# Moving one output projection inside every step of a software-pipelined attention and FFN kernel

## What is computed

```python
h = gelu(other @ W1 + readout @ W2 + b)                      # token layer
n = layernorm(h)
q, k, v = split(n @ qkv_w.T)                                 # 16 heads of 64
scores = q @ k.T * 64**-0.5 + bias[bucket(key - query)]      # T5 relative bias
h = h + (softmax(scores) @ v) @ o_w.T                        # attention
n = layernorm(h)
h = h + (silu(n @ wg.T) * (n @ wu.T)) @ wd.T                 # gated FFN, int weights / 127
```

## Time and profile before

| what | value |
|---|---|
| median of 3 runs | 1811.13 us (1810.99 to 1811.48) |
| the profiled execution's own time | 1811.56 us |
| its span, first to last instruction | 1809.3 us |
| granted TensorE clock, mean of the span | 0.99 |
| PE busy | 1766.2 us (98%) |
| PE weight loads busy | 1648.3 us (91%) |
| DVE, ACT, POOL busy | 1515.6 us (84%), 1396.9 us (77%), 1167.8 us (65%) |
| DMA queue of the loads and stores | 5.7% of 16 engines' span |
| chain that ended last | PE 95%, DVE 3%, ACT 1%, issue 1% |

### The profile page before, as it was taken

How to read it: one execution, slowest core, us unless ns; L and a number is a source line. 1 busy time by engine, 2 the same in 40 slices (tenths; PEclk the granted TensorE clock), 3 DMA queues, 4 the chain that set the end, 5 groups by cost and what they waited for, 6 DMA issues and landing times.

```text
span 1809.3 us, 47269 instructions
## 1 busy us (share of the span) xinstructions
PE 1766.2 (98%) x17434; PEld 1648.3 (91%) x17434; DVE 1515.6 (84%) x4828; ACT 1396.9 (77%) x3795; POOL 1167.8 (65%) x1488
## 2 busy tenths in 40 slices
PE   7899999999999999999999999999999999999996
PEld 5789999999999999999999999999999999999995
DVE  4888888888888888888888888888889888889884
ACT  4877778777778777787777787777787777877873
POOL 2566567666667666667666667666667666667664
PEclk8999999999999999999999999999999999999998
DMA  5200000000000000000000000000000000000000
GB/s 181 71 11 16 16 10 9 14 16 16 16 7 11 16 16 16 16 4 14 16 16 16 16 4 13 16 16 16 16 5 13 16 16 16 16 5 13 8 7 13
DMA packets 26761, 34.13 MB, mean 19 GB/s; under 512 B 3457, under 2 KB 20370, under 8 KB 26530
## 3 DMA queue, kind: packets, MB, share of 16 engines
q1 hardware_dynamic: 26368, 30.95, 5.7%
q10 hardware_dynamic: 98, 0.07, 0.0%
q0 software_dynamic: 64, 0.07, 0.0%
HBM read 22.65 MB, written 8.42 MB: 17 GB/s over the span
## 4 chain that ended last, share of the span: by engine, by line
PE 95%; DVE 3%; ACT 1%; issue 1%; POOL 0%; DMA 0%; POOLq 0%; ACTq 0%; DVEq 0%
PE ps L480 57%; PE ps L561 14%; PE ps L537 13%; PE ps L550 7%; PE ps L489 3%; PE ps L505 2%; DVE prob L958 1%; DVE pT L966 1%; ACT prob L786 0%; POOL normed L410 0%; ACT pT L793 0%; DMA emb_sb<-emb 0%; DVE wu L897 0%; ACT xt L753 0%; DVE v L944 0%
## 5 line engine op out<-in xcount | busy, mean ns | idle before, releaser
L419 POOL TENSOR_TENSOR prob<-prob,inv 128x510 f32<-128x510 f32 x512 | 524.8, 1039 | 371.6 <-DVE inv L971 371.6
L793 ACT ACTIVATE pT<-ps 128x512 fp32r<-128x512 f32 x512 | 278.5, 597 | 322.4 <-PE ps L550 322.3
L786 ACT ACTIVATE prob<-prob,neg_top 128x255 f32<-128x255 f32 x1024 | 506.8, 502 | 5.0 <-DVE neg_top L958 4.7
L958 DVE CUSTOM_DVE_ANT_0 prob<-ps,bias 128x255 f32<-128x255 f32 x1024 | 380.1, 420 | 98.8 <-PE ps L537 91.5
L480 PE MATMUL ps<-xnT,wqk 128*128 128x256 f32 x3072 | 417.0, 285 | 2.9 <-DVE qk L936 1.5
L480 PEld LDWEIGHTS ps<-xnT,wqk 128*128 128x128 f32 x3072 | 381.8, 189 | 15.2 <-issue 1.8
L966 DVE TENSOR_TENSOR pT<-ps,pT 128x512 fp32r<-128x512 f32 x512 | 334.5, 685 | 1.5 <-ACT pT L793 1.5
L561 PE MATMUL ps<-pT,v 128*128 128x256 f32 x2048 | 294.9, 287 | 20.3 <-DVE pT L966 11.2
L561 PEld LDWEIGHTS ps<-pT,v 128*128 128x128 f32 x2048 | 263.7, 190 | 37.6 <-issue 31.8
L537 PE MATMUL ps<-qk 64*128 64x256 f32 x3072 | 252.5, 297 | 0.8 <-DVE neg_top L958 0.8
L537 PEld LDWEIGHTS ps<-qk 64*128 64x128 f32 x3072 | 198.9, 186 | 35.7 <-issue 1.8
(11 more groups left out here) (93 smaller groups left out, 2592.0 us busy)
## 6 DMA issues: line engine op xcount, KB each, us to landing
xt<-x_cols SPq DMA_DIRECT2D x32, 256.0 KB, 2.6
out<-xt SPq DMA_DIRECT2D x32, 128.0 KB, 1.7
r_rows<-readout_rows SPq DMA_DIRECT2D x30, 128.0 KB, 2.9
out<-xt SPq DMA_DIRECT2D x32, 112.0 KB, 1.8
bias<-bias_rows SPq DMA_DIRECT2D x8, 384.0 KB, 4.2
staged<-w_qk SPq DMA_DIRECT2D x8, 256.0 KB, 4.3
staged<-w_v SPq DMA_DIRECT2D x4, 256.0 KB, 3.8
staged<-w_o SPq DMA_DIRECT2D x4, 256.0 KB, 4.9
```

Source lines behind the costliest of these rows:

```text
L419: pool.tensor_tensor(pr, pr, by, ALU.mult).then_inc(prob_done, 1)
L786: ex = act.activation(pr, pr, ACT.Exp, bias=neg_top[:, g % 2, hh, t:t + 1], scale=-1.0, accum_out=total[:, g % 2, hh, t:t + 1])
L793: act.activation(transposed(0, half), transposed_in(half), ACT.Copy).then_inc(pT_hi, 1)
L958: ins = dve.tensor_tensor_reduce(prob[:, g % 2, hh, t, 0:S], ps[:, bank_s[hh], t * T:t * T + S], falling(2 * g + hh, WINDOW - 1 - b0), 1.0 ...
```

## The change

In the step of the TensorE queue, the six lines with the projection of pair G-3 go from between `values_probs` and `scores` to between `probs_transposed` and `late()`. Nothing else is changed: no instruction, buffer, semaphore or other queue.

```diff
                         values_probs(*pair(G - 2))
-                    if pair(G - 3):
-                        bb, gg = pair(G - 3)
-                        if gg == 0 and bb > 0:
-                            pe.wait_ge(h1_done, count(1, bb - 1))
-                        project(bb, gg)
                     if pair(G):
                         score_banks_free()
                         scores(i, g)
                     if pair(G - 1):
                         transpose_banks_free()
                         probs_transposed(*pair(G - 1))
+                    if pair(G - 3):
+                        bb, gg = pair(G - 3)
+                        if gg == 0 and bb > 0:
+                            pe.wait_ge(h1_done, count(1, bb - 1))
+                        project(bb, gg)
                     late()
```

## The result

Slower by a quarter of a per cent: 1816.93 us as the median of 14 runs (1814.42 to 1818.37), against 1812.56 us for the kernel before (14 runs, 1810.84 to 1814.68); ratio 1.0025, 95% interval 1.0017 to 1.0033, so +4.5 us (3.1 to 6.0). The prediction on record was +4.7 us.

What follows compares the result with a forecast made beforehand. The prediction took TensorE (PE), busy 98% of the span, as the bound. Middle +7.1 us and ends -2.45 gave +4.7 on 1811.1, so 1815.8 us, range 1807 to 1825.

Steps and rivals of the forecast that it cites:

- In the middle it can only lose: Between the kernel's two ends, on a full PE, reordering removes no work; waits behind the projection lose its 0.71 us cover.
- The gap at g=0: PE's 0.11 us wait for DVE ahead of `values_probs`, costing about 0.35 us with refilling, expected to disappear.
- Scores at g=4, 0.18 us: Scores wait for DVE's `v_lo` of values 3 and start 0.18 us late, in 31 batches.
- hand-over of 0.15 us: Time from a DVE record's end to PE's first waiting matmul, read as 0.15 us (906.00 to 906.15).
- Transposes at g=4, 0.05 us: Head 1 of the transposes waits for POOL's second L419: 0 to 0.13 us, taken as 0.05 per batch.
- 0.29 forecast: POOL's string to the g=4 transposes starts 0.29 us sooner, since g=1's earlier transposes release ACT and DVE work.
- the rival: POOL doesn't move up: head 1 at g=4 costs 0.33 us, not 0.05; total 1824.5 us; chance 20%.
- Transposes at g=7, 0.30 us, paid back at g=0 by 0.35: Transposes wait 0.30 us for `gated_done` of tile 5; the next `values_probs` saves gap and refill, 0.35; net taken as 0.
- g=2 and g=6, nothing to spare: Scores waiting for `output` at g=2 and FFN tile 3 at g=6 are just in time: both cost 0.
- Middle 7.1 us: Loss between the ends: 31 batches times 0.18 us for scores plus 0.05 for transposes at g=4, +7.1 us.
- Ends -2.45 us: First steps gain 1.25 us as `add_bias` stops waiting for scores; the drain gains 1.2 without the projection ahead of transposes.
- By it PE has 9% to give: Weight loads fill 91% of PE; by that rule 0.2 us waits vanish, giving 1808.7 us; the prediction rejected it.

Runs made afterwards that it cites:

- 9: Kernel before, but in every step the projection's first token tile stays ahead of the scores and the second goes behind the transposes: 1809.95 us, ratio 0.9992.
- kernel 10: Kernel before, with the projection moved behind the transposes only at g=7, 0 and 1: 1808.38 us, ratio 0.9981 to the kernel before.
- 1: Kernel after, but at g=4 the projection stays ahead of the scores: 1811.52 us, ratio 0.9996 to the kernel before.
- 7: Kernel after, with ACT copying the FFN norm's hi part ahead of values 3 at g=4: 1841.48 us, ratio 1.0166 to the kernel before.
- 8: Kernel before, with ACT copying the FFN norm's hi part ahead of values 3 at g=4: 1826.59 us, ratio 1.0078.
- experiment 2: Kernel before, with the projection moved behind the transposes at g=4 alone: 1829.44 us, ratio 1.0095.
- 4: Kernel after, but at g=2 and g=4 the projection stays ahead of the scores: 1817.68 us, ratio 1.0026 to the kernel before.
- 3: Kernel before, with the projection moved behind the transposes at g=7 alone: 1810.60 us, ratio 0.9992.

## Why the prediction was right, and where it was not

- **"In the middle it can only lose"**: true of the change as a whole, period +0.17, and half a projection as cover removes all of it (9). As a rule it fell: the period of kernel 10 is 0.07 us below that of before, and 0.05 of it is `down` at a closer pace, which a sum of waits can't see. The gap at g=0 only paid for the wait at g=7.
- **Scores at g=4, 0.18 us**: right in place (1, 7, 8), too large in size: 0.10. The term that was mis-sized is the hand-over of 0.15 us, taken from one wait of `values_probs`. At these scores it is 0.06, and with that the prediction's own sum gives 935.25 against 935.16, so 0.09.
- **Transposes at g=4, 0.05 us**: 0.07. The size is right by two errors: POOL moved up by 0.40 for the 0.29 forecast, but the transposes also start 0.08 sooner than forecast. That POOL moves up at all hangs on the neighbouring steps, which experiments 2 and 4 showed at the price of the rival, 0.55 for 0.51.
- **Transposes at g=7, 0.30 us, paid back at g=0 by 0.35**: 0.25 and 0.26; net 0 as forecast (3). The same hand-over of 0.15 was in it, and is 0.05 here.
- **g=2 and g=6, nothing to spare**: the scores of neither are late, and with a hand-over of 0.05 they had 0.1 us more to spare than the prediction said. But the transposes of g=2, which the prediction didn't price, take 0.08 longer. They wait for POOL: its second result of that step is there at 924.78 + 1.04 = 925.82, and head 1 starts at 925.87, as late after it as in the named waits for POOL of experiment 2.
- **Middle 7.1 us**: 5.4. The over-large hand-over, 31 x 0.08 = 2.5 us, is more than the difference; the 0.08 at g=2 and the gains of 0.02 to 0.05 in steps that had no wait nearly cancel.
- **Ends -2.45 us**: about -1.3 by the times, from -2.9 to +0.4, and 0.7 and 0.8 by the traces. At the start both waits went, but what they cost did not: 0.7 of 1.25 was won, and a good part of the rest went into a weight piece that ran beside POOL. At the drain the mechanism was right, and 0.8 of 1.2 was won at an equal clock; two waits in the last batch, 0.2 and 0.6 us, were not in the sum.
- **"By it PE has 9% to give"** (the Trainium skill, page "Perfetto Trace Analysis", section "Identifying the Most-Contended Engine"): the trace disagrees. (The section speaks of the distance to the roofline and of headroom, and names the share of peak FLOPs beside that of the weight loads; that a wait fits into the 9% was the prediction's step.) On this PE, whose weight loads fill 91%, waits of 0.1 us at g=4 came out of the period when they were taken away (1), and an idle time of 0.25 us with what it brings with it made the period longer by 0.55, together with the scores' wait of 0.1 (2).

The forecast came out 0.2 us from the ratio's centre. It deserves less than that: its two parts were off by 1.7 and about 1.1 us, in opposite directions, and that they nearly cancelled is luck.

## What to carry to other kernels

Ask of an independent piece of work in a full queue what it covers: it is free to stay, and moving it costs the waits behind it, even of 0.1 us, times the number of repeats. Read the hand-over at more than one wait before it goes into a sum that is multiplied by 31: here one profile held 0.05 and 0.15, even for the same consumer. Test a move step by step, in neighbouring pairs too, since one step's earlier release may be what hides the next one's wait, and then mix: the best version here moves the piece in three steps of eight. Where profiles of one program differ in clock at the end, compare a pair in which the clock fell at the same place.

## What the runs showed of the hardware

- The time from the end of a DVE instruction to the start of the PE matmul that waited for it was, at full clock, 0.05 to 0.06 us at some waits and 0.14 to 0.15 at others, in one profile, and both for `values_probs` and for the scores. From POOL's end to a transpose it was 0.05 us (943.62 to 943.67 in experiment 2).
- A DVE subtraction over a tile of 128 x 256 took 0.92 to 0.95 us beside a running POOL subtraction (three profiles), and 0.42 us alone.
- Behind a gap of 0.11 us at full clock, the 8 matmuls of `values_probs` took 1.19 us in the chain, and 0.94 to 0.96 without one.
- In the drain the granted clock fell to 0.50 and rose again at places that differ between the profiles, for either order: at the last `values_probs` it was 0.50 in the kernels after, 2 and 3, and full in the kernels before and 7.
